# Attention scores from two float32r parts in half of the array's rows, with the score matmuls of a step paired

## The reference

```python
def _L0_conv_ref(x, Wq, bq, Wk, bk, Wv, bv, Wp, bp):
    ...
    xh = x.reshape(b_, HEADS, HEAD_DIM, n)          # 2 images, 8 heads, 16 channels, 1024 pixels
    q = proj(Wq, bq, xh)
    k = proj(Wk, bk, xh)
    v = proj(Wv, bv, xh)
    attn = jnp.einsum('bgdi,bgdj->bgij', q, k) * SCALE
    attn = jax.nn.softmax(attn, axis=-1)
    out = jnp.einsum('bgij,bgdj->bgdi', attn, v)
    out = proj(Wp, bp, out)
    return out.reshape(b_, c, h, w)
...
x = x + _L0_conv_ref(_gn(x), ...)
x = x + _L1_conv_ref(_gn(x), ...)
```

## Time and profile before

| | |
|---|---|
| median of three runs | 368.35 us (367.45 to 369.86) |
| the profiled execution | 367.55 us |
| its span in the trace | 365.6 us |
| PE busy | 309.8 us, 85% of the span |
| DVE busy | 258.9 us, 71% |
| ACT busy | 194.1 us, 53% |
| POOL busy | 103.9 us, 28% |

### The profile page before, as it was taken

One profiled execution on the slowest core, in us unless ns is written; L12 is line 12 of the kernel. 1 busy time (PEld: TensorE's weight loads), 2 busy tenths in 40 slices (PEclk: granted clock), 3 DMA queues, 4 the chain that ended last, 5 costly groups with the idle time before them and its releaser, 6 DMA issues.

```text
span 365.6 us, 5601 instructions
## 1 busy us (share of the span) xinstructions
PE 309.8 (85%) x2046; PEld 106.8 (29%) x2046; DVE 258.9 (71%) x270; ACT 194.1 (53%) x359; POOL 103.9 (28%) x137
## 2 busy tenths in 40 slices
PE   7568779999990599999989999998981999698796
PEld 2244123333320133333323333333220344222242
DVE  3746759898970177887748988879898146999820
ACT  1406347767760267767757666766760546453132
POOL 5000051111010011011000036999980100894410
PEclk9969699999995599999999999999995799969899
DMA  5168950000699300000000000590000001960001
GB/s 198 29 210 129 162 104 3 30 31 0 125 120 125 37 1 2 1 2 3 1 2 0 2 2 3 158 204 5 1 2 0 0 0 74 192 167 2 0 0 57
DMA packets 11022, 19.97 MB, mean 55 GB/s; under 512 B 2035, under 2 KB 2931, under 8 KB 10995
## 3 DMA queue, kind: packets, MB, share of 16 engines
q1 hardware_dynamic: 10998, 19.64, 26.6%
HBM read 13.61 MB, written 5.54 MB: 52 GB/s over the span
## 4 chain that ended last, share of the span: by engine, by line
PE 59%; DVE 20%; DMA 9%; issue 4%; SPq 3%; ACT 2%; POOL 2%; DVEq 0%; ACTq 0%; POOLq 0%
PE ps L971 15%; PE ps L930 15%; PE ps L960 12%; DVE qs L744 11%; DMA qs<-mrows 6%; PE ps L1122 4%; DVE mx L696 4%; DMA ks<-parts_dram 2%; PE ps L1136 2%; SPq L331 2%; PE ps L951 2%; PE ps L1081 2%; PE ps L876 2%; PE ps L902 1%; ACT pr L568 1%
## 5 line engine op out<-in xcount | busy, mean ns | idle before, releaser
L696 DVE TENSOR_REDUCE mx<-ps 128x1 f32<-128x1024 f32 x128 | 154.3, 1221 | 55.5 <-PE ps L930 51.0
L568 ACT ACTIVATE pr<-ps 128x512 f32<-128x512 f32 x256 | 139.0, 595 | 98.8 <-PE ps L960 98.7
L960 PE MATMUL ps<-qs,ks 99*128 99x512 bf16 x256 | 79.6, 389 | 17.8 <-DMA qs<-mrows 16.9
L930 PE MATMUL ps<-ks,qs 96*128 96x512 bf16 x256 | 79.4, 395 | 10.7 <-DMA ks<-part 5.5
L971 PE MATMUL ps<-pr,va 128*32 128x256 f32 x1024 | 83.5, 398 | 0.0
L744 DVE SCALAR_TENSOR_TENSOR qs<-xpad,w,qs 128x512 f32<-128x512 f32 (+1 forms) x35 | 54.7, 1562 | 1.0
L433 POOL TENSOR_TENSOR mparts<-zeros,mx 128x8 bf16<-128x8 f32 x16 | 3.7, 230 | 169.0 <-DVE mx L696 169.0
L960 PEld LDWEIGHTS ps<-qs,ks 99*128 99x128 bf16 x256 | 24.5, 99 | 61.2 <-DMA qs<-mrows 16.7
L971 PEld LDWEIGHTS ps<-pr,va 128*32 128x32 f32 x1024 | 20.3, 109 | 51.4 <-issue 46.8
L930 PEld LDWEIGHTS ps<-ks,qs 96*128 96x128 bf16 x256 | 17.0, 99 | 55.5 <-issue 44.2
L1056 PE MATMUL ps<-xr,wt 128*32 128x512 f32 x224 | 30.0, 664 | 3.5 <-DMA xr<-pad_dram 3.5
(11 more groups left out here) (99 smaller groups left out, 229.2 us busy)
## 6 DMA issues: line engine op xcount, KB each, us to landing
parts_dram<-part SPq DMA_DIRECT2D x12, 256.0 KB, 2.6
xr<-pad_dram SPq DMA_DIRECT2D x8, 361.0 KB, 6.2
qs<-parts_dram SPq DMA_DIRECT2D x6, 256.0 KB, 11.6
ks<-parts_dram SPq DMA_DIRECT2D x6, 256.0 KB, 15.8
xr<-pad_dram SPq DMA_DIRECT2D x4, 304.0 KB, 10.7
qs<-parts_dram SPq DMA_DIRECT2D x6, 192.0 KB, 4.9
ks<-parts_dram SPq DMA_DIRECT2D x6, 192.0 KB, 7.3
xr<-pad_dram SPq DMA_DIRECT2D x4, 285.0 KB, 10.3
```

Source lines behind the costliest of these rows:

```text
L568: nc.scalar.activation(pr[:, j % PR, c * HALF:(c + 1) * HALF], st[c], ACT.Exp, scale=SCALE).then_inc(exp_done, 1)
L696: nc.vector.tensor_reduce(mx[:, r, i:i + 1], sm[i % 2], AX.X, ALU.max).then_inc(max_done, 1)
L930: last = nc.tensor.matmul(sm[i % 2][:, c * HALF:(c + 1) * HALF], qs[0:STACK, bass.ds(s * N + i * P, P)], ks[0:STACK, bass.ds(s * N + c * H ...
L960: nc.tensor.matmul(st[c], ks[0:ROWS, bass.ds(t * N + j * P, P)], qs[0:ROWS, bass.ds(t * N + c * HALF, HALF)], start=True, stop=True).then_ ...
```

## The change

Queries and keys are split into two parts of type float32r instead of three of bf16. Three products of parts are summed, so the stack has 3 x 16 = 48 rows and, with two rows of maxima (the keys' side holds -1 there), 50. A head's stack takes half the array's rows: `rows_of(t)` puts heads 0, 1, 4, 5, ... on partitions 0 to 63 and heads 2, 3, 6, 7, ... on 64 to 127, and `cell_of(t)` gives one of two places in the free dimension. So `qs` and `ks` hold four heads and not sixteen. A head's stack is copied by six DMAs from SBUF to SBUF (`stack`, L338 of the changed kernel), and DRAM is no longer used for it. The stacks of heads 0 and 1 are issued by SP (queries) and ACT (keys), those of 2 and 3 by SP behind them. Each later one (`next_stack(t)`, heads 4 to 15) waits until the head that had its place is through with its `scores_t`, which is head t - 4.

The main loop on PE now works in pairs: `scores_t` is issued one step earlier than before, and each half of it is followed by one half of `scores`; `times_v` stands behind these four. `LAG` is 1, so that 15 tiles of `scores` precede the first head, and `scores` mostly belongs to head t + 2, in the other half of the rows. The loops over heads are unrolled. DVE no longer splits the parts of image 1 (POOL does it now), and of image 0 it computes only the low part. The maxima are split in two parts by two POOL instructions instead of five.

```diff
-PARTS = 3
-STACK = 6 * D
+PARTS = 2
+TERMS = 3
+STACK = TERMS * D
 ROWS = STACK + PARTS
-Q_ORDER = (0, 1, 2, 0, 1, 0)
-K_ORDER = (0, 0, 0, 1, 1, 2)
+GROUP_ROWS = 64
+CELLS = 2
+Q_ORDER = (0, 0, 1)
+K_ORDER = (0, 1, 0)
...
+def rows_of(t):
+    return t // 2 % 2 * GROUP_ROWS
+def cell_of(t):
+    return t % 2 * N
...
+        def stack(queue, i, t, n):
+            order, dst = ((Q_ORDER, qs), (K_ORDER, ks))[i]
+            queue.wait_ge(S(f"part{i}{n}", t // HEADS), 1)
+            h = t % HEADS
+            for g in range(TERMS):
+                if order[g] == n:
+                    queue.dma_start(
+                        dst[rows_of(t) + g * D:rows_of(t) + (g + 1) * D, cell_of(t):cell_of(t) + N].bitcast(F32),
+                        hl[h * D:(h + 1) * D, t // HEADS, i, n, :].bitcast(F32)).then_inc(S("stack", t), 16)
...
+            def next_stack(t):
+                sp.wait_ge(st_ready, 2 * NT * (t - 3))
+                for n in range(PARTS):
+                    stack(sp, 0, t, n)
+                    stack(sp, 1, t, n)
...
+            row_max(0)
+            for t in range(1, T):
+                if t + 3 < T:
+                    next_stack(t + 3)
+                row_max(t)
+                if t == FINISH + 3:
+                    replicate(0)
+            replicate(1)
...
+            def head(t, also=()):
                 for j in range(NT):
+                    n = NT * t + j
+                    here = plan[t][j]
+                    if n + 1 < NT * T:
+                        scores_t(n + 1, 0)
+                    if here:
+                        scores(*here[0], 0)
+                    if n + 1 < NT * T:
+                        scores_t(n + 1, 1)
+                    if here:
+                        scores(*here[0], 1)
+                    if n:
+                        times_v(n - 1)
```

More of the change, by code:

```diff
@@ L28 @@
 BF16 = mybir.dt.bfloat16
+F32R = mybir.dt.float32r
 ACT = mybir.ActivationFunctionType
@@ L385, in replicate @@
                             .then_inc(S(f"rep{h}", b), 16)
[L387 to L399, removed]
-            with sp.Fori(3, T // 2 - 1) as pair:
-                row_max(2 * pair, 0)
-                row_max(2 * pair + 1, 1)
-            replicate(0)
-            for s in range(T - 2, T):
-                row_max(s, s % 2)
+            row_max(0)
[5 more added lines that the diff above has]
+                    replicate(0)
             replicate(1)
@@ L569, in head @@
+                        nc.scalar.activation(pr[:, n % PR, c * HALF:(c + 1) * HALF], st[c], ACT.Exp,
                                              scale=SCALE).then_inc(exp_done, 1)
-                    if j == 0 and later(t, 1):
-                        copy_u(t - 1, 1 - r)
-                    if j == turn:
-                        copy_max(t + 1, 1 - r)
+                    if j == 0 and t:
+                        copy_u(t - 1)
+                    if j == max_turn(t) and t + 1 < T:
+                        copy_max(t + 1)
@@ L579, in copy_oc @@
                 nc.scalar.activation(oc[:, 0, :], sm[0], ACT.Copy).then_inc(S("oc", 0), 1)
-            copy_max(0, 0)
-            head(0, 0)
-            head(1, 1)
-            with a.Fori(1, FINISH // 2) as pair:
-                head(2 * pair, 0)
-                head(2 * pair + 1, 1)
-            for t in range(FINISH - 1, T - 2):
-                head(t, t % 2, turned(t), also={LAG: copy_oc} if t == FINISH else {})
+            copy_max(0)
+            for t in range(T - 2):
+                head(t, {LAG + 1: copy_oc} if t == FINISH else {})
             def ln_square(k):
@@ L964, in times_v, with scores_t @@
-            def times_v(t, r, j):
-                if j == 0:
-                    if later(t, 1):
-                        t_.wait_ge(u_ready, t)
-                t_.wait_ge(exp_done, 2 * NT * t + (2 * j + 2))
+            def scores_t(n, c):
+                t, j = divmod(n, NT)
+                if n:
+                    t_.wait_ge(exp_done, 2 * n + c - 1)
+                if j == 0 and c == 0:
+                    t_.wait_ge(s_mrow[t % 2], 16 * (t // 2 + 1))
+                rows = slice(rows_of(t), rows_of(t) + ROWS)
+                nc.tensor.matmul(st[c], ks[rows, cell_of(t) + j * P:cell_of(t) + (j + 1) * P],
+                                 qs[rows, cell_of(t) + c * HALF:cell_of(t) + (c + 1) * HALF],
+                                 start=True, stop=True).then_inc(st_ready, 1)
@@ L993, in head @@
                             function(*given)
-                    for s, i in plan[t][j]:
-                        scores(s, i)
+                    for s, i in here[1:]:
+                        scores(s, i, 0)
+                        scores(s, i, 1)
             def finish_turn():
@@ L1036, in _ @@
                     t_.wait_ge(S("copied1"), 1)
-                    turn_max(0, 0)
-            t_.wait_ge(S("kones"), 16)
+                    turn_max(0)
+            t_.wait_ge(S("kones"), 32)
             t_.wait_ge(S("va", 1), 1)
+            for c in range(2):
+                scores_t(0, c)
             also = {FINISH: [(LAG, finish_turn), (LAG + 2, finish_project)],
```

391 lines of the change are left out of this document (169 added, 222 removed).

## The result

The change makes the kernel much slower: 532.43 us in the median (528.11 to 536.55, four runs), against 369.11 for the kernel before on the same chip. The ratio is 1.438, with a 95% interval of 1.422 to 1.455. The profiled execution took 529.34 us, with a span of 527.5.

The account below looks back on a forecast made before the run. PE was taken to bound a step (1.54 us). Start 40.0, head 0 11.5, twelve heads of 17.35, then head 13, image 0's projection and the part behind gave a 402.05 us span, 405 us in all, range 376 to 440.

Parts of the forecast that it names:

- The queue: On SP, six stack DMAs stand ahead of the row maxima for heads 1 to 12; PE idles some 4.75 us each.
- What the clock does: Each of twelve waits for row maxima ends with PE's clock low, giving 4.4 us more of cold steps.
- E to R: From a head's last scores_t on PE to PE's restart after the row maxima: 5.65 us, bounds 4.6 and 6.3.
- the clock holds: Rival: PE's clock stays up through the waits for row maxima, giving 383 us; chance 0.09.
- R to E: From PE's restart after the row maxima to that head's last scores_t: 11.7 us.
- The cold step: A main-loop step on PE at the low clock: 1.97 us, with pairs at 2 x 0.43, switch 0.14, times_v 0.97.
- ACT's order: In each head, copy_u, copy_max and normalise find less room than before: 0.5 us.
- The pairs and float32r: Float32r score matmuls on PE take 0.22 us and run side by side in different rows; a warm step takes 1.28.
- the pairs don't pair: Rival: float32r matmuls take 0.43 us or rows don't run side by side, 436 us; both, over 500; chance 0.15 together.
- weights bind: Rival: a step's four float32 weight loads on PE follow one another uncovered, step 1.47 us, total 419; chance 0.12.
- The start: Before the heads, PE starts its scores at 18.5 us instead of 21.29, and the first scores_t at 40.0.
- Head 13's wait of 4.8: On SP, replicate(0) now stands ahead of head 13's row maxima, so PE waits 4.8 us there.

Follow-up runs that it names:

- experiment 2: Changed kernel with row maxima issued first and ACT's copies later, all heads in one half: 538.57 us over 48/50 rows, 393.56 us zero-padded to 96/98.
- experiment 3: Pairs zero-padded to 62/64 rows: 368.98 us in the changed kernel with row maxima issued first and ACT's copies later, 488.78 us in the changed kernel otherwise as is.
- experiment 5: Kernel before, with scores over rows 0 to 47 only and scores_t over 64 to 98, nothing else changed: 373.07 us, one run.

## Why the prediction was wrong

**The direction and the queue held; what the clock does behind each wait didn't, and the size with it.** Forecast were 405 us and a range to 440; measured 532. By the profiled spans, 402.05 was forecast and 527.5 came, 125.5 more. They lie as follows: 14.1 before the restart of head 1 (57.15 forecast, 71.21), 87.0 from there to the restart of head 12 (196.35 forecast, 283.34), 24.4 behind it.

**The queue: right.** E to R was to be 5.65 us and is 5.84, with PE idle for 4.83 (4.75 forecast), twelve times. The six issues take 3.7 us (142.73 to 146.44), that of the maxima and its landing the rest.

**What the clock does: the step that failed.** The forecast took from the start of the kernel before (a restart at 21.29, back at 25.6) and from head 5 that the clock is back 4.3 us after a restart. Both are restarts with matmuls of 96 rows and more. It carried this over to matmuls of 48 and 50 rows, for which no row of before existed, and gave it no bound. There it isn't back before the next restart in eight of twelve heads, though PE works for 19.4 us and more in each; in the others it is back after 4.3, 9.6, 13.4 and 21.9 us. Experiments 2 and 3 show that the row count decides much of this, and experiment 5 agrees; why the recovery varies between heads with the same instructions stays open. The rival "the clock holds" (0.09) looked only in the other direction, and none was for a clock that stays down. For a head whose R to E is 19.36 us (123.33 to 142.69), against 11.7: 5.3 steps that stay cold make 5.3 x 0.69 = 3.7.

**The cold step: mis-sized.** 1.97 forecast, 2.16 measured, mostly since the first pair of a step takes 0.59 and not 0.43. Over seven steps 1.3 us.

**ACT's order: mis-sized.** `copy_u` and `copy_max` were to cost 0.5 a head for want of room. The prediction saw that `scores_t` is a step earlier on PE, but not that ACT's copies keep their place and now wait for a `times_v` that is a step later relative to the exponentials. The order of ACT against PE's new one would have shown it. PE waits for it 0.99 and 0.83 us, 1.8 a head, and the edit alone is worth 25 us. PE's own transposes (`turn_u` 0.62 us, `turn_max` 0.38) had no term at all. So 3.7 + 1.3 + 1.8 + 1.0, less the forecast's 0.5, are 7.3 of the 7.7 us that R to E is longer in this head. In every second head two steps' `scores` fall in the same half and don't pair, some 0.85 us each (96.43 to 98.40 and 99.41 to 101.41), which makes 9.0 of 9.4.

**The pairs and float32r: right.** The rivals "the pairs don't pair" and "weights bind" fell. A warm step of the changed kernel, from the timeline:

```profile
240.94 0.50 PE L925 MATMUL ps<-qs,ks 50*128 50x512 f32 x1
240.94 0.50 PE L888 MATMUL ps<-ks,qs 48*128 48x512 f32 x1
241.27 0.39 PE L925 MATMUL ps<-qs,ks 50*128 50x512 f32 x1
241.28 0.39 PE L888 MATMUL ps<-ks,qs 48*128 48x512 f32 x1
241.60 0.64 PE L936 MATMUL ps<-pr,va 128*32 128x256 f32 x8
242.17 0.44 PE L913 MATMUL ps<-w,u 128*128 128x128 f32 x2
```

It takes 1.23 us, forecast 1.28. The first pair takes 0.33 and not 0.22 (the second's 0.33 has the 0.10 for the change to `times_v` in it), and that much was covered by the 1.25 us of ACT and DVE.

**The start: right in kind.** The first `scores` start at 21.62 (18.5 forecast: the keys' six issues on ACT take 0.70 each and land 3.7 us later) and the first `scores_t` at 48.82 (40.0), as the clock was at half from 17 to 34 and again from 44 on. Head 13's wait of 4.8 didn't come: the heads were so slow that the copies of the image had landed.

## What to carry to other kernels

Before you shorten the contraction of the matmuls that fill a kernel, ask what it does to the clock: look at the granted clock behind each wait, and don't carry a recovery time over from matmuls of another height. When one engine's work is moved by a step, move the places in every other engine's order that wait for it. And price the holes of the kernel before by themselves: here the one worth 17 us was had by moving twelve DMAs in a queue, and the rest of the change, taken together, cost more than it gave.

## What the runs showed of the hardware

- In this program PE's busy time didn't settle the clock, and the height of the matmuls counted: with 48 and 50 rows PE was busy without a pause from 60 to 290 us at 1.2 GHz, with the same instructions over 96 and 98 rows, half of them zeros, it ran at 2.4 GHz from 60 to 180. Height alone didn't settle it either: the second kernel was at 1.2 GHz from 48 to nearly 60 us under a busy PE, and pairs of 48 and 50 rows, once up, kept the clock up for 109 us until a wait of 1.64 us. How it is decided stays open: no run here varies the height finely.
- Float32r matmuls of 512 columns one after another start 0.43 us apart at the low clock (experiment 2, 48 and 50 rows) and 0.23 at the high one (96 and 98 rows); behind the first of a step it is 0.60 and 0.34. The first pair of a warm step takes 0.33 for both of its matmuls, no more than one alone. Its weight load took 281 to 290 ns in the changed kernel (most of it cold), the bf16 one before 99.
- Two matmuls in different rows overlapped by themselves, without any setting, when they followed each other in the queue, here into different PSUM banks: in the kernel before with few rows, `scores` and `scores_t` started 0.01 us apart.
